# Attention and experts in one kernel: ranks of pairs 19-22 read one projection earlier, and row scatters moved around the power instructions

## The reference, cut to what matters

```python
x = x + xattn(layernorm(x), ctx, ctx, mask, Wq, bq, Wk, bk, Wv, bv, Wo, bo)
xt = layernorm(x)                       # input of the second block
router_probs = softmax(xt @ Wr + br)
gates, idx = max(router_probs), argmax(router_probs)
xn = layernorm(xt) * ln_g + ln_b
h = relu(xn @ W1[idx] + b1[idx])
y = (h @ W2[idx] + b2[idx]) * gates
x = x + y
```

## Time and profile before

| what | us |
|---|---|
| median of 3 runs | 268.35 |
| the three runs | 268.5, 268.35, 265.58 |
| the profiled execution's own time | 268.41 |
| its span | 266.5 |
| mean granted TensorE clock | 0.976 of full |
| attention, up to the end of its last projection | about 165.6 |
| first matmul with expert weights | 181.9 |

### The profile page before, as it was taken

The page is one execution under the profiler, slowest core; times in us unless marked ns, Lnnn a source line. Parts: engine busy times, 40 slices in busy tenths (PEclk is TensorE's granted clock), DMA queues, the critical chain, the costliest instruction groups (busy, mean ns, idle before and its releaser), DMA issues.

```text
span 266.5 us, 9096 instructions
## 1 busy us (share of the span) xinstructions
PE 245.3 (92%) x3197; PEld 193.9 (73%) x3204; DVE 215.3 (81%) x690; ACT 171.3 (64%) x339; POOL 141.9 (53%) x170
## 2 busy tenths in 40 slices
PE   7699999999999999999989978887999999999960
PEld 2366685876777767858768666337999999999960
DVE  7776888998989989978978975734789999999950
ACT  2698886876967868768636441003588888888820
POOL 3764363438647865855595257730445455555550
PEclk9999999999999999999999997997999999999995
DMA  6789980000000000000001011144021222222100
GB/s 188 233 244 349 409 321 1 5 0 13 14 13 23 13 14 24 13 10 23 23 13 35 2 41 33 41 115 93 25 71 52 66 70 74 63 74 71 42 23 0
DMA packets 17483, 19.55 MB, mean 73 GB/s; under 512 B 2703, under 2 KB 13332, under 8 KB 17440
## 3 DMA queue, kind: packets, MB, share of 16 engines
q1 hardware_dynamic: 14016, 14.15, 16.9%
q0 software_dynamic: 2272, 4.27, 4.6%
q10 hardware_dynamic: 1152, 0.57, 0.8%
HBM read 14.11 MB, written 5.33 MB: 73 GB/s over the span
## 4 chain that ended last, share of the span: by engine, by line
PE 73%; DVE 12%; issue 5%; DMA 2%; ACT 2%; POOL 2%; another core or an unknown queue 1%; POOLq 1%; SPq 0%; DVEq 0%; ACTq 0%
PE ps L1215 14%; PE ps L1226 12%; PE ps L1035 9%; PE ps L1048 8%; PE ps L1141 7%; DVE Pr L836 4%; PE ps L1137 4%; PE ps L1074 4%; DVE mx L829 3%; PE ps L1020 3%; PE ps L1105 3%; PE ps L1208 2%; PE ps L1075 1%; PE ps L1061 1%; PE ps L1112 1%
## 5 line engine op out<-in xcount | busy, mean ns | idle before, releaser
L526 POOL DMA_INDIRECT out<-ot,G x39 | 37.9, 972 | 46.9 <-DVE ot L1004 28.5
L551 ACT ACTIVATE PT<-ps 128x512 f32<-128x512 f32 x64 | 34.7, 595 | 35.0 <-PE ps L1048 32.1
L829 DVE TENSOR_REDUCE mx<-ps 128x16 f32<-128x1024 f32 x32 | 39.2, 1224 | 12.7 <-PE ps L1141 12.2
L1035 PEld LDWEIGHTS ps<-VB,PT 128*64 128x64 f32 x1024 | 32.7, 138 | 13.7 <-issue 12.9
L469 POOL TENSOR_TENSOR Kb<-KT,hmask 128x512 f32<-128x512 f32 x32 | 33.2, 1039 | 16.5 <-PE ps L1141 14.4
L430 POOL DMA_INDIRECT rows_dram<-row,posi x32 | 32.7, 1023 | 15.5 <-issue 6.1
L598 ACT ACTIVATE Pr<-Pr,rowany 128x1024 f32<-128x1024 f32 x32 | 36.8, 1151 | 4.2 <-DVE Pr L836 4.0
L836 DVE TENSOR_TENSOR Pr<-ps,mx 128x1024 f32<-128x1024 f32 x32 | 38.9, 1215 | 0.1
L1035 PE MATMUL ps<-VB,PT 128*64 128x18 f32 x1024 | 36.0, 212 | 1.6 <-issue 0.8
L1048 PE MATMUL ps<-ident,Pr 128*128 128x128 f32 x256 | 34.7, 278 | 0.2 <-issue 0.2
L1215 PE MATMUL ps<-xg,WR 128*128 128x128 f32 x248 | 32.8, 275 | 0.0
(11 more groups left out here) (133 smaller groups left out, 423.2 us busy)
## 6 DMA issues: line engine op xcount, KB each, us to landing
WA<-in_wpk SPq DMA_DIRECT2D x8, 578.0 KB, 9.5
G<-rows_dram SPq DMA_DIRECT2D x39, 66.0 KB
X<-in_x SPq DMA_DIRECT2D x8, 256.0 KB, 6.5
C<-in_ctxT SPq DMA_DIRECT2D x8, 256.0 KB, 6.5
XT<-in_xT SPq DMA_DIRECT2D x8, 256.0 KB, 6.6
out<-ot,G POOLq DMA_INDIRECT x39
rows_dram<-row,posi POOLq DMA_INDIRECT x32
rows_dram<-empty ACTq DMA_DIRECT2D x6, 66.0 KB, 1.6
```

The source lines that it names most:

```text
L526: g.indirect_dma_start(out=out, out_offset=bass.IndirectOffsetOnAxis(ap=G[:, q, D + 1:D + 2].bitcast(I32), axis=0), in_=ot[:, q, :], in_of ...
L551: a.activation(PT[:, p % 2, 512 * m:512 * m + 512], ps[:, 4 + m, :], ACT.Copy).then_inc(freed[4 + m], 1)
L829: v.tensor_reduce(out=mx[:, i % 2, :], in_=psS.rearrange("p g (i k) -> p g i k", k=S), axis=AX.X, op=ALU.max).then_inc(s_mx, 1)
L1035: last = mm(pv_ps(p)[64 * b:64 * b + 64, 18 * j:18 * j + 18], PT[:, p % 2, 128 * j + 64 * b:128 * j + 64 * b + 64], VB[:, p // GP % 3, 2 * ...
```

## The change

Four edits. First, the ranks of unit 5 are put beside `o0` of unit 6 (bank 6) instead of `o1` (bank 7), so that they can be read one projection earlier; TensorE's order stays as it was. Second, on DVE, in step 29, reading the ranks of unit 5, its places and its gate move ahead of and between the residual and moments of unit 6. Third, in step 31, DVE reads ranks, places, gate and count of unit 6 ahead of the residual of unit 7, not behind its variance. Fourth, POOL's order of scatters and powers from unit 5 on is another, with two waits more.

```diff
+        def ranked_with(u):
+            if not shares(u):
+                return ("r", u)
+            return ("o0" if u == NU - 4 else "o1", u + 1)
+
         def await_ranked(eng, u):
-            await_filled(eng, *(("o1", u + 1) if shares(u) else ("r", u)))
+            await_filled(eng, *ranked_with(u))
...
             if shares(u):
-                return ps[:, bank_of("o1", u + 1), 448:448 + E * UNITS[u][1]]
+                return ps[:, bank_of(*ranked_with(u)), 448:448 + E * UNITS[u][1]]
...
             scored(NP - 3)
             send(NU - 5, [2, 3])
+            send(NU - 4, [0, 1])
             rstd2(NU - 3)
             token_ids(NU - 3)
             scored(NP - 1)
-            send(NU - 4, [0, 1, 2, 3])
+            send(NU - 4, [2, 3])
+            pool.wait_ge(filled[5], NP)
             send(NU - 3, [0])
             rstd2(NU - 2)
             token_ids(NU - 2)
-            send(NU - 3, [1, 2, 3])
+            await_filled(pool, last_o(NU - 1), NU - 1)
+            send(NU - 3, [1])
             rstd2(NU - 1, 1, 2)
             rstd2(NU - 1, 0, 1)
             token_ids(NU - 1)
+            send(NU - 3, [2, 3])
             send(NU - 2, [0, 1])
             send(NU - 1, [0, 1, 2])
...
+                if (u := unit_at(i, "ranks")) is not None and u != NU - 3:
+                    read_ranks(u)
                 if i == NP - 3:
                     residual(NU - 3, 0)
-                    stats2(NU - 3, 0)
-                if (u := unit_at(i, "ranks")) is not None and u != NU - 3:
-                    read_ranks(u)
-                if i == NP - 2:
                     places(NU - 4)
                     gate(NU - 4)
+                    stats2(NU - 3, 0)
+                if i == NP - 2:
                     seen(NU - 4)
                 if i == NP - 1:
                     pick(NU - 3)
                     one_hot(NU - 3)
                     normalise(i - 2)
+                    read_ranks(NU - 3)
+                    places(NU - 3)
+                    gate(NU - 3)
+                    seen(NU - 3)
...
-            read_ranks(NU - 3)
-            places(NU - 3)
-            gate(NU - 3)
-            seen(NU - 3)
             normalise(NP - 2)
...
-                claim(*(("o1", u + 1) if shares(u) else ("r", u)))
+                claim(*ranked_with(u))
```

## The result

| what | before | after |
|---|---|---|
| median of 20 runs on this chip, us | 267.74 | 268.67 |
| lowest and highest, us | 265.58, 268.5 | 267.79, 269.93 |
| ratio after to before, 95% interval | | 1.0065 [1.0041, 1.009] |
| profiled execution, us | 268.41 | 269.34 |
| mean granted clock in it | 0.976 | 0.978 |

By the ratio the changed kernel is 0.65% slower (0.4 to 0.9); the two medians are 0.93 us or 0.35% apart, the means 0.57%. The range of the forecast holds the measured time, but the forecast was no change, and there is one.

A forecast was written before the change was run, and what follows sets the result against it. POOL's last scatter was taken to bound the kernel; +0.3 + 0 + 0 - 2.5 + 2.6 + 0.1 - 0.4 = +0.1 gave 268.5 us, a second way 268.2. Forecast 268.3 us, no change, range 267.1 to 269.0, chance 0.5.

The forecast's parts named there:

- Ranks of unit 5 earlier, +0.3: DVE, step 29: three instructions come ahead of pair 30's maximum, costing +0.3 us, bounds 0 and +0.4.
- Two scatters of unit 5 ahead of the powers of unit 6, 0: POOL: scatters 0 and 1 fit into idle time before these powers, cost 0; without that cover 2 x 1.3 us.
- The stall and its low clock, -2.5: TensorE, pairs 30 and 31 to last projection: splitting the scatter burst saves 1.8 us of stall, 0.7 of clock; bounds 0, -2.9.
- Wait for the last projection, +0.1: POOL: scatter 1 of unit 6 waits for it, just fitting before the variance; +0.1 us, bounds 0 and +0.3.
- Two scatters more behind the powers, +2.6: POOL's end: five scatters behind the powers of unit 8 become seven, at 1.3 us each; +2.6 us, bounds +2.6 and +2.7.
- Landing, -0.4: Last scatter, later against ACT's issues of empty blocks, meets less and lands faster; -0.4 us, bounds 0 and -1.0.
- Sum up to the first load of rows: All terms from DVE's ranks to the last scatter's landing add to +0.1 us, taken as no change.
- what bounds the kernel now: Attention's end to first expert block: POOL's last scatter sets the end; a microsecond there is a microsecond of the kernel.
- The stall stays: Rival, pairs 30 and 31: scatters don't cause the stall, it remains and the kernel is slower, 271.2 us; chance 0.25.
- The three scatters at 163 to 167 also held the engines, faster: Rival, last projections: moving scatters out of that chain gives back up to 2 us more, 266.3 us; chance 0.1.
- The clock stays low: Rival, last projections: stall goes but TensorE's clock stays low and landing slow, losing 0.7 and 0.4, 269.4 us; chance 0.1.

The follow-up runs named there:

- first pair: The kernel before and the changed kernel, 20 runs each on the first chip: medians 267.74 and 268.67 us, ratio 1.0065.
- e4: Kernel before with scatters 2 and 3 of unit 6 sent behind the powers of unit 8, nothing else: 267.63 us, ratio 1.0144.
- e5: Changed kernel with 50 idle matmuls behind the last count in place of 36: 264.69 us, ratio 1.0038 to the kernel before.
- r4_after: The changed kernel once more, unaltered, in the sixth batch: 267.88 us, ratio 1.0057 to the kernel before.
- e10: Changed kernel with POOL's order and waits of before and 40 idle matmuls in place of 36: 266.48 us, ratio 1.0026 to the kernel before.
- r4_ahead: e1 once more, in the sixth batch: 263.87 us, ratio 0.9922 to the kernel before.
- e2: Changed kernel with POOL's order and waits of before, so only rank places and DVE's order differ: 263.13 us, ratio 0.9968 to before.
- e8: Kernel before with DVE's step 31 edit alone (ranks, places, gate, count of unit 6 ahead of unit 7's residual): 262.73 us, ratio 0.9986.
- r2_old_pool: e2 once more, in the third batch: 262.96 us, ratio 0.9989 to the kernel before.
- r3_old_pool: e2 once more, in the fourth batch: 262.98 us, ratio 0.9991 to the kernel before.
- e1: Changed kernel with scatters 1 to 3 of unit 6 ahead of unit 8's powers, no wait for the last projection: 263.22 us, 0.9982 to before.
- r2_ahead: e1 once more, in the third batch: 262.74 us, ratio 0.9982 to the kernel before.
- r2_after: The changed kernel once more, unaltered, in the third batch: 267.19 us, ratio 1.0125 to the kernel before.
- e7: Changed kernel with one unit 6 scatter behind unit 8's powers, two ahead, no wait for the last projection: 264.81 us, 1.0026 to before.
- r3_after: The changed kernel once more, unaltered, in the fourth batch: 266.55 us, ratio 1.0133; its profiled run took 264.40 us.
- e9: Kernel before with 50 idle matmuls between the last count and the first expert block in place of 36: 265.28 us, ratio 1.0078.
- fifth batch: e10 beside the kernel before, on a chip of its own: 266.48 us against a median of 265.3 for the kernel before.
- last batch: Sixth batch, r4_ahead and r4_after beside the kernel before on a chip of its own: 263.87 and 267.88 us against 265.6.

## Why the forecast was wrong

Point by point, on the first pair's profiles:

- *Ranks of unit 5 earlier, +0.3*: right. The maximum of pair 30 starts at 148.70, was 148.42.
- *Two scatters of unit 5 ahead of the powers of unit 6, 0*: right on POOL, wrong on its neighbours. They brought the 1.0 us wait at 149.92; the subtraction of pair 30 starts at 151.42 against 150.04, +1.38, of which 0.28 is the term above and 1.1 the wait. The sum had no term for it.
- *The stall and its low clock, -2.5*: right in sign, too small. The reading was too wide: DVE ran again from 157.67, 0.5 us before the burst was over, and only TensorE and ACT were held to 159.1 and 159.2. From the start of pair 31's transposes to the end of the products went from 161.49 - 156.43 = 5.06 to 160.88 - 157.81 = 3.07, -2.0 (-1.8 forecast). From there to the end of the last projection, 165.57 - 161.49 = 4.08 became 163.79 - 160.88 = 2.91, -1.2 (-0.7). Together -3.2, against +1.4 ahead of it: the last projection ends 1.8 us earlier (forecast 2.2).
- *Wait for the last projection, +0.1*: the variance is done at 165.36, the powers start at 165.68, 0.32 behind; before it was 167.21 - 167.12 = 0.09. +0.2.
- *Two scatters more behind the powers, +2.6*: from the powers to the last scatter 175.67 - 165.68 = 9.99, was 174.63 - 167.21 = 7.42. +2.57, right, as a delay of POOL.
- *Landing, -0.4*: from the last scatter's start to the load of rows 2.56, was 3.45. -0.9, inside its bounds, but not for the reason given. ACT's issues of empty blocks, which were to be over sooner, took 7.71 us instead of 6.07 and lasted to 178.28, past the landing. In the profiles of the batches it took 2.3 to 3.15 us with five scatters behind the powers and 2.3 to 2.5 with seven, so a short landing comes without two scatters more, too.
- Sum up to the first load of rows: (165.68 - 167.21) + 2.57 - 0.89 = +0.15, forecast +0.1. That this is so near is in part luck, since the missing +1.1 was made up for by two terms that came out larger.

**The step that failed** is in "what bounds the kernel now": everything behind 178 us is a pipeline that starts when these rows come, so that a microsecond at the last scatter is a microsecond of the kernel. It isn't. The row of idle matmuls starts with the last count, which doesn't wait for POOL, and ends at a time of its own. On the first pair rows and first block came as early as before and still +0.93 was lost: the end of attention had come 1.8 us earlier, and with it the end of that row (1.5 us earlier), TensorE's idle time grew from 2.11 to 3.38 us, and the low clock came sooner and stayed longer. On a chip without the stall e4's two scatters are +1.9 on POOL and +3.8 in time. What is lost behind the first block's start is the clock's, on e5's showing: filling the idle time gives 2.0 us back, with the same scatters in the same places. The filling was tried on one chip without the stall, and not on one with it; and r4_after, with an idle time of 3.42 us, still has a clock of 0.96 from 180 to 182, so the length of the idle time doesn't by itself say when the clock falls.

**The baseline** was the second fault. The sum was counted from one profiled execution of the upper group, with the stall and with the low clock behind it, and the run at 265.58 was taken for one without the stall. e10 speaks against that: its lowest run has the stall and the full clock. From the end of the products, 161.49 in both profiles, the last projection ends at 164.70 in e10 and at 165.57 before, 0.9 us of low clock; the sum had 0.7. e10 has VectorE's new order, four more idle matmuls and another chip, so whether the low runs of the first pair had the stall stays open. The absolute forecast, 268.3, lies 0.4 us from the measured 268.67, and that is luck: with 20 runs the kernel before came down from 268.35 to 267.74.

How large the difference is goes with the chip: +0.65% and +0.57% on two chips whose kernel before ran at 267.7 and 265.6, +1.1, +1.25 and +1.3% in three batches, on two chips, where it ran at 263.4 to 263.8. The first two show the large stall or the 1.0 us wait in a profile, the others neither. That the stall makes the difference isn't shown apart from what else sets these chips apart.

**The rivals.** *The stall stays* did not come true: the three profiles with split scatters on such chips (after, r4_after, r4_ahead) lack it, and both with the burst (before, e10) show it. These are few profiles on three chips, and one chip alone has both kinds. e10 has VectorE's new order, so that isn't what removes it; the split and the wait for pair 31's transposes came together in all three, and which of the two does it wasn't tried. What in the chip holds the engines isn't shown either; in before and e10 no packet of an instruction queue lies between 156 and 160 us. The Trainium skill ("DMA: Bandwidth & Descriptors", "Queues, rings and completion order") has each DMA engine switch between its queues packet by packet; no run here shows what the queues did to each other. The time that the prediction put beside it, 271.2, did not come out. *The three scatters at 163 to 167 also held the engines, faster* is out: r4_ahead has them there (162.22 to 165.83), and its last projection ends 2.89 us behind the products, against 2.90 in r4_after, which has one from 164.70 on. *The clock stays low*, 269.4, is the rival nearest in number, to the 268.67 and to the profiled 269.34, but named the wrong place: the clock was full in the last projections and low in the first expert blocks.

**What the parts are worth.** VectorE's edits with POOL's old order: medians 0.4 to 0.7 us under before on the chips without the stall (e2, e8, r2_old_pool, r3_old_pool), but only e2 is clear of no change, and e8 has one of the two edits alone. The split of unit 5's scatters: nothing without the stall (e1 against e2, r2_ahead against r2_old_pool, 0.1 and 0.2 us), and perhaps the main part of the 2 us of r4_ahead; there was no kernel in that batch with VectorE's part and the burst, so the share isn't measured. The scatters behind the powers: 3.8 us in e4 against before, 4.4 and 4.0 us in after against r2_ahead and r4_ahead, with the wait for the last projection in it. e1 is the version to keep: it was no slower than before on the three chips that it ran on, and 0.8% faster on the one with the 1.0 us wait.

**Open:** what makes the clock fall in some runs and not in others, and with it what the upper group of times is on the chips of the first pair and the last two batches; which part of the change removes the stall; and whether the 1.0 us wait can go too, say with one scatter at a time there; the latter wasn't tried.

## What to carry to other kernels

A filler of fixed length in front of a stage is a clock of its own: when you move what it covers, or what starts it, compute both ends anew, and look at the granted clock behind the gap, not only at the gap. A delay is not priced by its length alone: with rows 2.2 us later r2_after took 4.8 us more than r2_ahead, and more than half of it was the clock. And before an edit is priced by a stall in one profiled run, profile a run of each group: a low run among three can have the same stall and another clock.

## What the runs showed that I had not expected

- **More idle work, less time.** 14 more idle matmuls in after, 3 us of them, gave 264.69 for 266.66 us; the same 14 in the kernel before cost 1.9 us. The Trainium skill, "TensorE: Matmul & The Clock Gate", Part 1 on the clock gate, says that the throttled state is the default and that activity releases it. The rows agree in that the clock was low behind idle time (2.11 us in before, 2.25 in e7, 3.15 in r2_after); but r3_after kept it full behind 3.01, and e9 lost it behind gaps of 0.73 and 0.89, which r3_old_pool (0.74 and 0.89) did not, so the length of a gap alone doesn't tell.
- **A stall that goes with some chips and with a burst.** With four scatters in a row ACT stood still for 2.71 us (before) and 2.58 us (e10), with no release that the profile can name; DVE for 1.40 and 2.73, and TensorE for 0.84 and 0.55 in the middle of its products. With two and two there is a wait of 1.0 us, where the first two now are. The large one was seen on two chips (the first pair's and the fifth batch's), the small one on the first pair's and the last batch's, and neither in the 15 profiles of the first four batches.
- **Idle matmuls at half speed.** In the profiles of e1 and e2 the row of 36 took 9.63 us, and 7.94 in r2_ahead, the same kernel as e1 on another chip: their own clock moves the end of the filler by 1.7 us.
